# A decoder layer for two batches in turn on one core: a new order of steps that sets the batches further apart

## The reference, cut to what matters

```python
x = x + _L0_attn_ref(_layernorm(x), Wqkv, bqkv, Wout, bout)            # rope, 16 heads, 256 keys
x = x + _L0_xattn_ref(_layernorm(x), ctx_1024, Wq, bq, Wk, ..., bo)    # 16 heads, 77 keys
x = x + _L0_ffn_ref(_layernorm(x), ew, act_w, We, be, Wq, ..., ln_b)
# _L0_ffn_ref: six nodes in a row; node c is an attention of 8 heads over 256 keys whose
# q, k, v come from earlier nodes:
for c in range(NUM_NOD):
    q = ew[c, 0] * (nodes[in_q] @ We[eq] + be[eq])
    k = ew[c, 1] * (nodes[in_k] @ We[ek] + be[ek])
    v = ew[c, 2] * (nodes[in_v] @ We[ev] + be[ev])
    o = _mha(q, k, v, Wq[c], Wk[c], Wv[c], Wo[c])
    nodes[c] = act_w[c] * o + q
```

## Time and profile before

| | |
|---|---|
| median of 3 runs | 5447.38 us (5445.13 to 5449.93) |
| the profiled execution's own time | 5450.77 us |
| its span, first to last instruction | 5449.0 us |
| PE busy | 5088.6 us, 93% of the span |
| DVE, ACT, POOL busy | 51%, 46%, 12% of the span |
| mean granted TensorE clock | 0.953 |
| one turn of the loop | 327.7 us |
| start of the first turn on PE | about 206 us |

### The profile page before, as it was taken

One profiled execution on the slowest core, in us unless ns is written; L12 is line 12 of the kernel. 1 busy time (PEld: TensorE's weight loads), 2 busy tenths in 40 slices (PEclk: granted clock), 3 DMA queues, 4 the chain that ended last, 5 costly groups with the idle time before them and its releaser, 6 DMA issues.

```text
span 5449.0 us, 155972 instructions
## 1 busy us (share of the span) xinstructions
PE 5088.6 (93%) x64256; PEld 3743.1 (69%) x64256; DVE 2799.5 (51%) x5095; ACT 2516.2 (46%) x4784; POOL 656.1 (12%) x1756
## 2 busy tenths in 40 slices
...
GB/s 124 7 2 10 3 2 11 2 11 2 8 5 2 11 2 10 3 2 11 2 10 3 8 5 2 11 2 10 3 2 11 2 10 3 6 7 2 11 2 8
DMA packets 45096, 46.93 MB, mean 9 GB/s; under 512 B 11969, under 2 KB 44097, under 8 KB 44353
## 3 DMA queue, kind: packets, MB, share of 16 engines
...
## 4 chain that ended last, share of the span: by engine, by line
PE 51%; issue 35%; DVE 5%; POOL 3%; ACT 2%; POOLq 0%; ACTq 0%; DVEq 0%
PE banks L893 50%; DVE row_max L863 3%; PE banks L1010 1%; ACT probs L773 1%; POOL neg_max L679 1%; POOL neg_max L682 1%; POOL inv_std L658 1%; DVE q_parts L835 0%; PE banks L940 0%; DVE rope_s L832 0%; POOL var_eps L655 0%; ACT k_parts L731 0%; DVE k_parts L841 0%; DVE rope_s L828 0%; ACT q_parts L721 0%
## 5 line engine op out<-in xcount | busy, mean ns | idle before, releaser
L863 DVE TENSOR_REDUCE row_max<-banks 128x4 f32<-128x1024 f32 (+1 forms) x1293 | 1327.7, 1070 | 774.2 <-PE banks L893 738.4
L773 ACT ACTIVATE probs<-banks 128x1024 f32<-128x1024 f32 (+1 forms) x1288 | 1139.2, 935 | 598.2 <-PE banks L893 596.7
L893 PE MATMUL banks<-k_parts,q_parts 32*128 32x256 f32 x12472 | 525.2, 299 | 173.0 <-DVE row_max L863 67.2
L893 PEld LDWEIGHTS banks<-k_parts,q_parts 32*128 32x128 f32 x12472 | 423.9, 189 | 325.1 <-issue 219.2
L893 PE MATMUL banks<-node_t,w_n 128*128 128x256 f32 x2560 | 637.4, 391 | 5.5 <-ACT node_t L790 5.5
L893 PE MATMUL banks<-q_parts,k_parts 32*128 32x256 f32 x12384 | 526.9, 302 | 38.2 <-DVE row_max L863 31.9
L893 PEld LDWEIGHTS banks<-q_parts,k_parts 32*128 32x128 f32 x12384 | 423.6, 192 | 200.4 <-issue 128.1
L893 PEld LDWEIGHTS banks<-node_t,w_n 128*128 128x128 f32 x2560 | 462.6, 189 | 123.9 <-issue 39.5
L679 POOL TENSOR_TENSOR neg_max<-row_max,zeros 128x8 fp32r<-128x8 f32 x645 | 143.5, 222 | 3341.1 <-DVE row_max L863 3336.6
L764 ACT ACTIVATE max_rows<-banks 128x256 fp32r<-128x256 f32 x514 | 195.2, 383 | 657.3 <-PE banks L1010 657.2
L783 ACT ACTIVATE context_t<-banks 128x256 f32<-128x256 f32 x514 | 198.1, 385 | 639.3 <-PE banks L893 639.0
...
## 6 DMA issues: line engine op xcount, KB each, us to landing
x_next<-in_x SPq DMA_DIRECT2D x34, 256.0 KB, 2.7
out_y<-x_tok SPq DMA_DIRECT2D x32, 256.0 KB, 2.1
...
w_edge_t<-in_we_t ACTq DMA_DIRECT2D x10, 256.0 KB, 12.0
w_edge_t<-in_we_t SPq DMA_DIRECT2D x10, 256.0 KB, 11.6
...
w_n<-in_we ACTq DMA_DIRECT2D x3, 256.0 KB, 11.5
```

What stands on the lines that cost most here:

```text
L773: done(act.activation(probs[s][0:rows, g % 2, 2 * p:2 * p + 2, 0:kt, :] .rearrange("p c k t -> p c (k t)"), psum[0:rows, b0:b0 + 2, 0:kt * T],
L863: done(dve.reduce_max(row_max[s][:, g, 2 * p:2 * p + 2, :].rearrange("p c q -> p (c q)"), psum[:, b0:b0 + 2, :].rearrange("p c (q t) -> p ...
L893: return nc.tensor.matmul(bank_ap, lhs, rhs, start=start, stop=stop, **kw)
```

## The change

Only the table `ORDER` changes. It holds the same steps for a turn; where each stands, its bank and which steps carry a + differ. No instruction's shape changes.

```diff
 ORDER = """
-XB0.1 +LOADX0 MX1.0.2.1 SB1.0.3 MX1.0.3.0 MX1.0.3.1 S0.1.0@4 SB0.1.0 MX0.1.0.0 MX0.1.0.1 NM1.0.2 S0.1.1@0
...
-+SB1.0.0 +MX1.0.0.1 +VE1.0 +S1.0.1@0 +SB1.0.1 +MX1.0.1.1 +MX1.0.0.0 +MX1.0.1.0 +S1.0.2@4 +SB1.0.2 +S1.0.3@0
-+XB1.0 +NM1.0.0 +MX1.0.2.0
++LOADX0 KR1.0@5 KC1.0 EX0.1.1.0 EX0.1.1.1 ST0.1.2@0 SX0.1.2 EX0.1.2.0 EX0.1.2.1 KS1.0 PV0.1.1 +LNS0.0 KH1.0
...
++ST0.1.1@0 +XB1.0 +QH1.0.1 +KI1.0 +SX0.1.1 +QL1.0.1 +PV0.1.0@6
 """
```

127 lines of the change are left out of this document (64 added, 63 removed).

## The result

The changed kernel takes 5671.5 us (median of four runs, 5668.5 to 5678.6), the kernel before 5448.7 us on the same chip. The ratio is 1.041 with an interval of 1.039 to 1.043, so the change costs 223 us. The forecast was 5601 us and slower; the sign holds and the waits came where they were expected, the size is 70 us too small, because work at the low clock was underrated.

A forecast was written before the change was run, and what follows sets the result against it. TensorE was taken as the bound: 302 us a turn of full-speed work, 27 of waits and 8 of slow clock made 337.0, 9.3 over 327.7. Sixteen turns (149) plus 5 for the start gave 5601 us, range 5400 to 5705.

The forecast's parts named there:

- The first place: SELF of slot 1, around the loop's jump: TensorE waits of 12.0 us a turn where 9.3 stood.
- (c): From KR1.0 to S1.0.0: TensorE idle 1.6 us while other engines prepare the keys.
- (e): PV1.0.0 in SELF of slot 1 waits as before, 0.5 us.
- (d): Eight maxima of SELF of slot 1, with score steps sharing banks 0 to 3: TensorE idle 6.8 us.
- The seven places: Waits elsewhere in the turn, made by bank numbers or queues: together 10.9 us, or 5.5 at the low end.
- Small pieces: Small TensorE waits elsewhere in the turn: 4 us allowed for the new order.
- The slow clock: Time a turn lost to TensorE's lower clock: left at 8 us, bounds 3 and 12.
- The start: Pass ahead of the loop: score steps sharing banks uncovered, 5 us once, bounds -5 and +12.
- The signs: Expected in the profile: 337 us turns, 1 to 2.5 us maxima waits, 2.7 us idle before a rope matmul, clock near 0.95.
- Faster by interleaving: Rival: attention-heavy stages beside the other slot's nodes let TensorE run through; 321.9 us a turn, 5360 us; chance 0.22.
- No difference: Rival: places only exchange, waits shrink from 27 to 18 us, clock the same; 5452 us; chance 0.06.
- The late load: Rival: x loads late behind XB1.0's wait for the store, delaying VectorE's layer norm and keys; 5676 us; chance 0.10.

The follow-up runs named there:

- after_seam: The changed kernel with the loop's jump moved on by 40 steps, into S1.0.3 as in the old order: 5593.1 us, ratio 1.026 to the kernel before.
- before_places: The kernel before with three second-half PVs of slot 1 put directly behind their exponent steps: 5656.1 us, ratio 1.037.

## Why the forecast was right in kind and short in size

- *Bound and prices.* Right within 2 us a turn. The work at full speed hardly changed: taking 41% off the busy time at the low clock (21.9 us a turn before, 33.6 after, from the traces' clock stretches) leaves 300.9 and 302.5 us. No order came near the floor that the weight loads' 227 to 230 us a turn would set.
- *The first place.* The mechanism was right and the size was off: 12.0 forecast, 8.5 measured in the turn shown (Q1.0 0.47; jump 2.84; 0.65; then 0.55, 0.66, 1.67, 0.52, 0.60 and 0.52). The jump's 2.7 in full and Q1.0's 0.4 came out. Parts (c), 1.6, and (e), 0.5, did not appear, and (d) is 4.5 for 6.8. What fell short is that I priced TensorE's steps there at the full clock; at the low one they cover the waits. The first turn shows the price at the full clock: (d) is 1.35, 1.37, 1.76, 0.52, 0.61 and 0.52, together 6.1 for the 6.8 of the forecast, and (c) 0.7 for 1.6. In the other turns it is no gain: what was not waited was worked slowly.
- *The seven places.* Right in kind at all seven; 10.9 forecast, 8.0 measured: PV1.3.1 0.93 and nothing at PV1.3.0; PV1.1.0 1.56; Q1.7 1.52; PV0.6.0 1.38; S0.0.3 0.93; S1.1.3 0.97; Q1.1 0.69. Only PV1.3.1 is far off: 0.69 us had been waited ahead of ST1.3.1, and PV1.3.0, which came later than I had it, did not have to wait for S0.5.0's maxima.
- *Small pieces.* 4 forecast, 7.6 measured; the largest that I had overlooked is TR1.2, 1.29 us every turn behind exponentials, 20.6 us in all in the waits shown.
- *Waits in sum.* +9.1 a turn forecast against the old 17.9, +6.3 measured.
- *The slow clock.* This is the term that was wrong. I left it at 8 us with bounds of 3 and 12, with the reason that the new order waits more but spread. Busy time grew by 6.4 us a turn, 102 us over the loop. By the estimate of 41% the loss is 9.0 before and 13.8 after, outside my upper bound, which leaves 1.6 of the 6.4. The 41% is a score step's; half an OB takes 1.13 us at the full clock and 2.07 at the low one, a loss of 45%, so with OB, and PV behind it, in the slow stretch the estimate is too low. What the runs show instead: in this order the term hangs on the stall at the jump and on what lies behind it. With the jump moved (after_seam) all of the 6.4 us are gone, 7.0 us a turn, though the waits are more; in the first turn, with no stall ahead, the low-clock time is 12 us. The spread waits, of which I had thought, can cost clock time too (4.0 us a turn for 9.2 us of waits in before_places, the old order), but in the new order no run shows that they do.
- *The start.* +5 forecast, +15 measured, 3 us above the upper bound.
- *The sum.* 102 us of clock, less 45 for the waits (2.8 a turn), plus 10 for the start are 67 us, where the spans' difference exceeds the 154 forecast by 65; the rest is rounding. That 5601 lies as near as it does is in part luck, since the waits were put too high and the clock too low.
- *The signs.* The wait ahead of the rope matmul (2.84 us) and the idle time (24.1 us a turn) came as named. Turns are 340.4 us for 337, the clock is 0.939 for 0.95, and the waits for the maxima (0.55 and 0.66 us) and for the exponentials at PV1.3.1 (0.93) are shorter than named.
- *The rivals.* Faster by interleaving: it needed waits and clock loss under 25.7 us a turn, and they are 38. The Trainium skill (Perfetto Trace Analysis, "Optimization Strategy") says that interleaving regimes may improve a kernel; this change does not bear that out. The score and exponent steps of both slots came next to each other and took all eight banks: by their bank numbers PV1.1.0, PV0.6.0 and Q1.7 wait for a bank to be read, and PV1.3.1 for its own exponentials. No difference: refuted. The late load: refuted above.

With the jump moved, 7.5 us of waits a turn remain over the kernel before (25.3 against 17.8). How much of them belongs to which of the seven places was not tried one by one. The halved exponentials take 1.1 us a turn off the difference in waits; that the banks are the cause of the rest is argued from the order, and no run shows it.
